# A pre-norm block on one core: first tiles by an uncentred W_in, two idle PSUM banks, three more tiles' statistics on ScalarE

## The chip, the core and the metric

The kernel runs on one core of one Trainium2 chip. A core has TensorE (PE, matrix products), VectorE (DVE), ScalarE (ACT), GpSimd (POOL) and SyncE (SP, which here only issues transfers). The metric is the device time of one execution in microseconds, lower is better.

## The reference

x is 4096 rows of 512, a context is 3202 rows of 1024, a mask has 3202 counts. Two blocks follow each other; everything is float32.

```
h      = rmsnorm(layernorm(x), g_res) @ W_in.T + b_in        # 512 x 512
c      = rmsnorm(context, g_init)[:, :512]
s      = a decaying scan of c along its rows                 # s[i] = a s[i-1] + b c[i]
x      = x + h + s[plug]        # plug: row of s for each row, from the mask's cumulative sums
x      = x + gelu(layernorm(x) @ w1 + b1) @ w2 + b2          # 512 -> 2048 -> 512
```

The layernorm and the rmsnorm in front of W_in are joined: a row's mean is taken out by centring W_in once (the mean over its input rows, weighted with g_res, is subtracted), so the product can be made from raw x, and the scale `ra` of each row is applied afterwards. Each float32 product is made of three float32r products: high x high, high x low, low x high, where a high part is a rounded copy and a low part is the rest.

## The kernel before

The order of work on each engine is written out by hand; engines meet only at semaphores.

The first half runs over 32 tiles of 128 rows (index t, `project(t)`, twelve products each). For a tile: TensorE transposes it in four 128x128 pieces into a bank (`transpose_first`, L847; three banks in turn), ScalarE copies the bank as its high part `h_hi` (`tile_high`, L687), VectorE makes the low part `h_lo` (`tile_low`, L1040), TensorE does the products into one of three banks `p_bank` (L859 to L861), and VectorE adds the scaled result to x (`tile_add`, L1048). Each tile's variance comes from `tile_stats`, on VectorE (L1035, L1036) or, for the tiles in `ON_ACT`, on ScalarE (three ACTIVATEs, L695 to L699); GpSimd makes the scales `ra` for two or four tiles at a time (L519, L520). `project(t)` of TensorE is one step; in ScalarE's and VectorE's loops step t holds the high and low parts of tile t+2, `tile_add(t-1)`, and statistics of a tile further on (t+6 on ScalarE, t+4 on VectorE).

In front of the loop stand 14 warm-up transposes (L887), the column sums of W_in as four fp32 products with a matrix of g_res (`g_wide`, `sum_w_in`, L854), the scaled copies `win_g` (L725), the centring on VectorE (L1140), and W_in's high (L729) and low parts (two on VectorE, L1145, two on GpSimd, L570). All products of the first three tiles wait for these.

Between the tiles lies other work, tied to steps: the mask's cumulative sums and "one-hot" matrices on VectorE (`mask_parts` to `one_hots_p`), which TensorE turns into counts (`mask_totals`, L896; `count_positions`, L902, 26 small products at step 16; `count_before`, L908), the squares and scales of the context on ScalarE (L703 to L712), its multiplication by g_init on GpSimd (L544) after the small loads (`small_loaded`: g_init, b_in, b2, b1), and the scan on VectorE with its carry from TensorE (`carry`, L891, `add_carry`, L1072). PSUM has eight banks: `t_bank` 0 and 1, `h_bank` 0 and 1, `acc` 0 to 3.

The second half does eight groups of 512 rows, 16 pieces of the hidden layer each, TensorE being full; the first group also splits w1 and w2 into parts.

SyncE's queue loads W_in first, then the mask, tiles 2 to 7, context rows and further tiles; ScalarE's queue loads g_res and tiles 0 and 1.

## Time and profile before

| | |
|---|---|
| median of 3 runs | 837.85 us (837.53 to 838.92) |
| profiled execution | 837.43 us, of which the span of the trace is 835.7 us |
| instructions | 10792 |
| TensorE products | 826.4 us busy, 99% of the span |
| VectorE, ScalarE, GpSimd | 315.2, 294.5, 256.3 us busy |

Busy times of TensorE overlap, since each product is recorded from entry to end, so its products are read by the distance between their starts. For the other engines too the distance from one start to the next is what an instruction costs in a full queue; the recorded duration is some 0.1 us longer. "idle before" is the time in which the engine had nothing to do, with what ended it.

### The profile page before, as it was taken

Reading aid. Unit: us, or ns where it says so; the run is one execution under the profiler, and the core shown is the slowest. Engines: PE = TensorE matmul, PEld = TensorE weight load, DVE = VectorE, ACT = ScalarE, POOL = GpSimd, SP = SyncE. Lnnn points to the kernel's source line nnn. Section 1 sums busy time; section 2 is a strip of 40 time slices with the busy share of each in tenths; the row PEclk is TensorE's granted clock in tenths of the full one; section 3 lists DMA queues with packets and bytes.
Section 4 is the critical chain, followed back from the end, with each engine's and each line's share of the span. In section 5 each row is a group of like instructions: output and inputs, shape, how many; then the busy total and the mean of one; then the engine's idle time right before and its main releaser. Section 6 shows DMA issues by size and latency. Waiting matters only on the chain.

```text
span 835.7 us, 10792 instructions
## 1 busy us (share of the span) xinstructions
PE 826.4 (99%) x3770; PEld 680.8 (81%) x3770; DVE 315.2 (38%) x513; ACT 294.5 (35%) x542; POOL 256.3 (31%) x236
## 2 busy tenths in 40 slices
PE   8999999999999999999999999999999999999998
PEld 5887888788888888888888888888888888888886
DVE  6899661664241333233332423143113311242112
ACT  5667446432622253224422262222222322222221
POOL 2273538950533026301631062305300250001000
PEclk9999999999999999999999999999999999999999
DMA  9858984251226022601233113302300230010001
GB/s 239 256 169 276 259 264 179 88 148 27 76 88 174 0 75 77 169 15 66 72 110 89 50 48 113 50 0 102 51 0 1 89 62 0 0 51 0 1 1 50
DMA packets 37327, 74.95 MB, mean 90 GB/s; under 512 B 6176, under 2 KB 6176, under 8 KB 35536
## 3 DMA queue, kind: packets, MB, share of 16 engines
q1 hardware_dynamic: 28324, 62.81, 23.3%
q0 software_dynamic: 4608, 8.39, 6.3%
q10 hardware_dynamic: 4368, 3.42, 1.4%
q8 instruction: 14, 0.23, 0.1%
q14 instruction: 13, 0.11, 0.0%
HBM read 47.87 MB, written 22.84 MB: 85 GB/s over the span
## 4 chain that ended last, share of the span: by engine, by line
PE 85%; POOL 4%; DVE 4%; DMA 2%; issue 2%; SPq 1%; ACT 1%; ACTq 0%; DVEq 0%; POOLq 0%
PE acc L859 14%; PE acc L861 14%; PE acc L860 14%; PE h_bank L859 14%; PE h_bank L861 13%; PE h_bank L860 13%; DMA xa_odd<-in_x_dram 2%; PE t_bank L918 2%; POOL w_lo L525 1%; POOL x_cur L624 1%; POOL cl L544 1%; DVE h_lo L1040 1%; POOL w_lo L531 1%; DVE st_a L1035 1%; SPq L348 0%
## 5 line engine op out<-in xcount | busy, mean ns | idle before, releaser
L1265 DVE TENSOR_TENSOR h_lo<-g_f,h_hi 128x512 fp32r<-128x512 f32 x128 | 99.9, 781 | 430.3 <-ACT g_f L796 420.9
L794 ACT ACTIVATE h_hi<-h_bank,b_c 128x512 fp32r<-128x512 f32 x128 | 88.2, 689 | 430.6 <-PE h_bank L861 425.7
L859 PE MATMUL h_bank<-xt_hi,w_hi 128*128 128x512 f32 x512 | 199.9, 390 | 0.6 <-POOL w_lo L525 0.6
L859 PE MATMUL acc<-w_hi,h_hi 128*128 128x512 f32 x512 | 199.8, 390 | 0.0
L861 PE MATMUL h_bank<-xt_hi,w_lo 128*128 128x512 f32 x512 | 199.3, 389 | 0.0
L860 PE MATMUL h_bank<-xt_lo,w_hi 128*128 128x512 f32 x512 | 199.2, 389 | 0.0
L861 PE MATMUL acc<-w_hi,h_lo 128*128 128x512 f32 x512 | 199.2, 389 | 0.0
L860 PE MATMUL acc<-w_lo,h_hi 128*128 128x512 f32 x512 | 199.2, 389 | 0.0
L859 PEld LDWEIGHTS h_bank<-xt_hi,w_hi 128*128 128x128 f32 x512 | 96.1, 188 | 20.7 <-issue 1.0
L861 PEld LDWEIGHTS h_bank<-xt_hi,w_lo 128*128 128x128 f32 x512 | 96.1, 188 | 20.0
L861 PEld LDWEIGHTS acc<-w_hi,h_lo 128*128 128x128 f32 x512 | 96.1, 188 | 20.0
L860 PEld LDWEIGHTS acc<-w_lo,h_hi 128*128 128x128 f32 x512 | 96.1, 188 | 19.7
L860 PEld LDWEIGHTS h_bank<-xt_lo,w_hi 128*128 128x128 f32 x512 | 96.1, 188 | 19.7
L859 PEld LDWEIGHTS acc<-w_hi,h_hi 128*128 128x128 f32 x512 | 96.1, 188 | 19.7
L796 ACT ACTIVATE g_f<-h_bank,b_c 128x512 f32<-128x512 f32 x128 | 87.4, 683 | 0.4 <-DVE h_lo L1265 0.4
L557 POOL DMA_INDIRECT x_next<-scan_table,idx x32 | 51.4, 1607 | 71.2 <-DMA scan_table<-cl 58.5
L544 POOL TENSOR_TENSOR cl<-cl,g_init_b 128x512 f32<-128x512 f32 x24 | 31.9, 1336 | 98.1 <-ACT ch L705 92.2
L624 POOL TENSOR_TENSOR x_cur<-x_next,b_b 128x512 f32<-128x512 f32 x32 | 44.1, 1408 | 58.4 <-DMA out_dram<-x_cur 58.0
L562 POOL TENSOR_SCALAR va_b<-mv_b 128x4 f32<-128x4 f32 x8 | 1.6, 197 | 176.9 <-DVE mv_b L1171 176.9
L552 POOL TENSOR_TENSOR x_next<-x_next,b_in_b 128x512 f32<-128x512 f32 x32 | 45.7, 1428 | 32.9 <-DMA x_next<-x_part 29.3
L859 PE MATMUL acc<-win_hi,h_hi 128*128 128x512 f32 x88 | 36.8, 418 | 1.8 <-DVE win_lo L1145 1.6
L861 PE MATMUL acc<-win_hi,h_lo 128*128 128x512 f32 x88 | 34.6, 393 | 0.0
(164 smaller groups left out, 695.8 us busy)
## 6 DMA issues: line engine op xcount, KB each, us to landing
out_dram<-x_cur SPq DMA_DIRECT2D x32, 256.0 KB, 2.1
x_next<-x_part SPq DMA_DIRECT2D x7, 1024.0 KB, 5.1
w_raw<-in_L_ffn_w_dram SPq DMA_DIRECT2D x6, 1024.0 KB, 9.1
scan_table<-cl SPq DMA_DIRECT2D x6, 896.0 KB
ch<-in_ctx_dram SPq DMA_DIRECT2D x20, 256.0 KB
cl<-in_ctx_dram SPq DMA_DIRECT2D x5, 1024.0 KB
xa_odd<-in_x_dram SPq DMA_DIRECT2D x16, 256.0 KB, 6.5
x_part<-xa_odd SPq DMA_DIRECT2D x16, 256.0 KB, 4.7
```

The source lines that it names most:

```text
L525: pool.tensor_tensor(w_lo[:, k, r], w_raw[:, k, r], w_hi[:, k, r].bitcast(F32), ALU.subtract).then_inc(w1_ready, 1)
L544: pool.tensor_tensor(rows[:, j, :], rows[:, j, :], g_init_b[:], ALU.mult).then_inc(g_scaled, 1)
L552: step(pool.tensor_tensor(x_next[:, i, :], x_next[:, i, :], b_in_b[:], ALU.add))
L557: pool.indirect_dma_start(x_next[:, i, :], None, rows, bass.IndirectOffsetOnAxis(ap=idx[:, i:i + 1].bitcast(U32), axis=0), compute_op=ALU. ...
L624: ins = pool.tensor_tensor(x_cur[:, i, :], x_next[:, i, :], b2_b[:], ALU.add)
L794: act.activation(h_hi[:, m % HB, :], h_bank[m % 2][:], ACT.Gelu, bias=b1_c[:, m:m + 1])
L796: act.activation(g_f32[:], h_bank[m % 2][:], ACT.Gelu, bias=b1_c[:, m:m + 1]).then_inc(gelu_done, 1)
L859: nc.tensor.matmul(dst, a_hi, b_hi, start=first, stop=False)
L860: nc.tensor.matmul(dst, a_hi, b_lo, start=False, stop=False)
L861: return nc.tensor.matmul(dst, a_lo, b_hi, start=False, stop=final)
L918: ins = nc.tensor.transpose(t_bank[i % 2][:, k * P:(k + 1) * P], n_rows[:, i, k * P:(k + 1) * P], ident[:])
L1265: dve.tensor_tensor(h_lo[:, m % HB, :], g_f32[:], h_hi[:, m % HB, :].bitcast(F32), ALU.subtract).then_inc(h_split, 1)
```

## The change

Tiles 0 to 2 (`RAW = 3`) are projected with a W_in that is scaled by g_res but not centred; it has its own high and low parts, `first_hi` (ScalarE, straight from the loaded block) and `first_lo` (VectorE). What the missing centring leaves is put right by a row operation on VectorE, `fix_tile`: x plus the negated column sums times mean times scale. GpSimd makes the products of mean and scale (`mean_scales`), and now adds up the four scaled blocks (`add_w_in`), so TensorE has one product with a matrix of ones instead of four (`sum_w_in`). ScalarE copies the negated sums to SBUF (`neg_sums`), from where W_in is centred for the tiles from 3 on. All four low parts of W_in are VectorE's. The loads of x tiles 0 to 2 and of W_in are interleaved over both queues. Tiles 3 and 4 are accumulated in `acc[3]` and `h_bank[0]`; `mask_totals`, which uses `h_bank[0]`, moves from step 4 to step 6 and waits for tile 4's add. Tiles 7, 9 and 11 get their statistics on ScalarE. The mask's steps on VectorE move by one (the first by two), the carry of the first context block moves from step 15 to 16 with its adds, warm-ups go from 14 to 10.

```diff
-WARM = 14
+WARM = 10
+RAW = 3
-ON_ACT = (6, 8, 10, 18, 20, 21, 22, 23, 24, 25, 26, 27)
+ON_ACT = (6, 7, 8, 9, 10, 11, 18, 20, 21, 22, 23, 24, 25, 26, 27)
+        def sums_bank(t):
+            return {3: acc[3], 4: h_bank[0]}[t] if t in (3, 4) else p_bank[(t + 2 * (t < 3)) % 3]
...
# SyncE
-            for k in range(K):
+            for t, k in ((0, 0), (1, 3)):
+                sp.dma_start(xa(t), x_v[0, :, t, :]).then_inc(xa_loaded[t], 16)
                 sp.dma_start(win_raw[:, k, :], win_v[:, k, :]).then_inc(win_loaded[k], 16)
+            sp.dma_start(xa(2), x_v[0, :, 2, :]).then_inc(xa_loaded[2], 16)
...
# GpSimd, before scales(0, 2)
-            for k in (2, 3):
-                pool.wait_ge(win_hi_done, k + 1)
-                pool.tensor_tensor(win_lo[:, k, :], win_raw[:, k, :], win_hi[:, k, :].bitcast(F32),
-                                   ALU.subtract).then_inc(win_lo_late, 1)
+            add_w_in(1)
+            add_w_in(2)
+            add_w_in(3)
             scales(0, 2)
+            mean_scales(0, 2)
             scales(2, 2)
+            mean_scales(2, 1)
...
# ScalarE
+            high_first(0)
             tile_high(0)
+            high_first(1)
+            scale_w_in(0)
+            scale_w_in(1)
+            tile_high(1)
+            high_first(2)
+            scale_w_in(2)
+            high_first(3)
+            scale_w_in(3)
+            tile_high(2)
+            act.wait_ge(win_summed, 1)
+            act.activation(neg_sums[:], acc[3][:], ACT.Copy, scale=-1.0).then_inc(neg_sums_made, 1)
             high_w_in(0)
-            tile_high(1)
-            high_w_in(1)
-            tile_high(2)
-            high_w_in(2)
-            high_w_in(3)
             tile_high(3)
+            for k in range(1, K):
+                high_w_in(k)
+            tile_high(4)
+            tile_high(5)
...
-                if 2 <= t < NT - 2:
+                if 4 <= t < NT - 2:
                     tile_high(t + 2)
...
# TensorE
             warm_up()
-            sum_w_in(0)
-            sum_w_in(1)
             transpose_first(0)
-            sum_w_in(2)
-            sum_w_in(3)
+            project_raw(0, 0)
             transpose_first(1)
+            project_raw(0, 1)
+            project_raw(1, 0)
+            project_raw(1, 1)
+            project_raw(0, 2)
+            project_raw(1, 2)
             transpose_first(2)
+            project_raw(0, 3)
+            project_raw(1, 3)
+            sum_w_in()
             transpose_first(3)
+            for k in range(K):
+                project_raw(2, k)
             transpose_first(4)
             for t in range(3, NT):
                 if t + 2 < NT:
                     transpose_first(t + 2)
-                if t == 4:
+                if t == 6:
+                    pe.wait_ge(acc_read, 5)
                     mask_totals()
-                if t == 15:
+                if t == 16:
                     pe.wait_ge(consts_made, 5)
                     carry(0, cl, acc[3][:])
...
# VectorE
+            def fix_tile(t):
+                dve.wait_ge(mean_ra_ready, t + 1)
+                ins = dve.scalar_tensor_tensor(x1(t), neg_sums[:], mean_ra[:, t:t + 1], xa(t), ALU.mult, ALU.add)
+                fixed.append(own.inc(ins))
...
-                for v in (t + LEAD,) if t < 22 else (2 * t - 18, 2 * t - 17) if t < 25 else ():
+                for v in {0: (), 1: (), 2: (4,), 3: (5,)}[t] if t < LEAD else (t + LEAD,) if t < 22 else (2 * t - 18, 2 * t - 17) if t < 25 else ():
```

VectorE before, from tile 2's low part (`h_lo<-acc`) to the statistics of tile 3 (BN_STATS, BN_AGGR); the centring and two low parts of W_in are done by then, and the first add follows soon after:

```order
L1040 TENSOR_TENSOR h_lo<-acc,h_hi 128x512 [waits x_hi]
L1035 BN_STATS st_a<-xa_even 128x6 [waits xa_loaded0]
L1036 BN_AGGR mv_a<-st_a 128x2 [waits dve_self]
L1035 BN_STATS st_a<-xa_even 128x6 [waits xa_loaded1]
L1036 BN_AGGR mv_a<-st_a 128x2 [waits dve_self]
L1040 TENSOR_TENSOR h_lo<-t_bank,h_hi 128x512 [waits x_hi]
L1035 BN_STATS st_a<-xa_even 128x6 [waits xa_loaded2]
L1036 BN_AGGR mv_a<-st_a 128x2 [waits dve_self]
L1035 BN_STATS st_a<-xa_even 128x6 [waits xa_loaded3]
L1036 BN_AGGR mv_a<-st_a 128x2 [waits dve_self]
```

VectorE in the changed kernel, behind the statistics of tile 3: centring (`win_raw<-neg_sums`), low parts of W_in and of tiles 3 to 5, fix rows, first add:

```order
L1194 SCALAR_TENSOR_TENSOR win_raw<-neg_sums,win_g 128x512 [waits win_scaled,neg_sums_made]
L1194 SCALAR_TENSOR_TENSOR win_raw<-neg_sums,win_g 128x512 [waits win_scaled]
L1204 TENSOR_TENSOR win_lo<-win_raw,win_hi 128x512 [waits win_hi_done]
L1194 SCALAR_TENSOR_TENSOR win_raw<-neg_sums,win_g 128x512 [waits win_scaled]
L1204 TENSOR_TENSOR win_lo<-win_raw,win_hi 128x512 [waits win_hi_done]
L1083 TENSOR_TENSOR h_lo<-t_bank,h_hi 128x512 [waits x_hi]
L1194 SCALAR_TENSOR_TENSOR win_raw<-neg_sums,win_g 128x512 [waits win_scaled]
L1204 TENSOR_TENSOR win_lo<-win_raw,win_hi 128x512 [waits win_hi_done] x2
L1083 TENSOR_TENSOR h_lo<-t_bank,h_hi 128x512 [waits x_hi]
L1083 TENSOR_TENSOR h_lo<-acc,h_hi 128x512 [waits x_hi]
L1091 SCALAR_TENSOR_TENSOR x_next<-neg_sums,mean_ra,xa_even 128x512 [waits mean_ra_ready] x3
L1102 SCALAR_TENSOR_TENSOR x_next<-h_bank,ra,x_next 128x512 [waits dve_self,ra_ready,h_used]
```

The centring, which stood in front of the statistics of tiles 0 to 3, now stands behind them, together with all four low parts, the low parts of tiles 3 to 5 and the three fix rows; the first add follows only then.

ScalarE before, from tile 3's high part to tile 7's:

```order
L687 ACTIVATE h_hi<-t_bank 128x512
L740 DMA g_init_b<-in_L_xattn_g_init_dram 128x512
L740 DMA b_in_b<-in_L_xattn_b_in_dram 128x512
L740 DMA b_b<-in_L_ffn_b_dram 128x512
L741 DMA b_c<-in_L_ffn_b_dram 128x16x1
L695 ACTIVATE g_f_59,sum_x<-xa_even 128x512
L697 ACTIVATE sum_x<-sum_x 128x1
L699 ACTIVATE g_f_59,mv_a<-xa_even,sum_x 128x512
L687 ACTIVATE h_hi<-t_bank 128x512
L695 ACTIVATE g_f_59,sum_x<-xa_odd 128x512
```

ScalarE in the changed kernel, from tile 5's high part on (statistics of tile 9 and tile 6's high part at the end):

```order
L719 ACTIVATE h_hi<-acc 128x512
L785 DMA g_init_b<-in_L_xattn_g_init_dram 128x512
L785 DMA b_in_b<-in_L_xattn_b_in_dram 128x512
L785 DMA b_b<-in_L_ffn_b_dram 128x512
L786 DMA b_c<-in_L_ffn_b_dram 128x16x1
...
L727 ACTIVATE g_f_59,sum_x<-xa_odd 128x512
L729 ACTIVATE sum_x<-sum_x 128x1
L731 ACTIVATE g_f_59,mv_a<-xa_odd,sum_x 128x512
L719 ACTIVATE h_hi<-t_bank 128x512
```

The high parts of tiles 4 and 5 moved ahead of the small loads, and the statistics of tiles 6 to 9 stand in one piece behind them, ahead of tile 6's high part; before, a tile's high part stood between any two of them.

## Rows read from the trace of the kernel before

**Rows 1.** The page: busy time of each engine.
```profile
PE 826.4 (99%) x3770; PEld 680.8 (81%) x3770; DVE 315.2 (38%) x513; ACT 294.5 (35%) x542; POOL 256.3 (31%) x236
```

**Rows 2.** Waits of TensorE, 0 to 205 us: total us, times, longest.
```profile
PE h_bank L859 <- POOL w_lo L525: 0.6, 1, 0.6
PE h_bank L908 <- DVE row_tot L1154: 0.2, 1, 0.2
```

**Rows 3.** Timeline of TensorE, 0 to 13 us: start, us, what.
```profile
2.53 3.25 PE L887 MATMUL acc<-ident 128*128 128x128 f32 x14 [2.53 <-POOL iota_p L504]
5.57 2.83 PE L854 MATMUL acc<-win_raw,g_wide 128*128 128x512 f32 x4
8.24 0.60 PE L847 MATMUL t_bank<-ident,xa_even 128*128 128x128 f32 x4
8.68 1.88 PE L854 MATMUL acc<-win_raw,g_wide 128*128 128x512 f32 x4
10.40 0.60 PE L847 MATMUL t_bank<-ident,xa_even 128*128 128x128 f32 x4
...
12.82 0.47 PE L859 MATMUL acc<-win_hi,h_hi 128*128 128x512 f32 x1 [1.39 <-DVE win_lo L1145]
```

**Rows 4.** Timeline of TensorE: transposes of two tiles that follow each other.
```profile
35.90 0.60 PE L847 MATMUL t_bank<-ident,xa_odd 128*128 128x128 f32 x4
...
39.11 0.60 PE L847 MATMUL t_bank<-ident,xa_odd 128*128 128x128 f32 x4
```

**Rows 5.** Timeline of SyncE's queue: issue of W_in's four blocks.
```profile
0.82 1.83 SPq L340 DMA_DIRECT2D win_raw<-in_L_xattn_W_in_dram  x4
```

**Rows 6.** W_in's tile: landings of its four blocks.
```profile
DMA to landing us min/median/max: 3.4/4.7/6.3
```

**Rows 7.** Timeline of VectorE, 15 to 38 us.
```profile
15.59 0.69 DVE L1035 BATCH_NORM_STATS2 st_a<-xa_even 128x6 f32<-128x512 f32 x1
...
16.48 0.67 DVE L1035 BATCH_NORM_STATS2 st_a<-xa_even 128x6 f32<-128x512 f32 x1
...
22.64 0.17 DVE L1078 TENSOR_SCALAR part_i<-mask_i 128x26 int32<-128x26 int32 x1
...
24.33 0.69 DVE L1035 BATCH_NORM_STATS2 st_a<-xa_even 128x6 f32<-128x512 f32 x1
...
34.22 0.75 DVE L1048 SCALAR_TENSOR_TENSOR xa_even<-h_bank,ra,xa_even 128x512 f32<-128x512 f32 x1
34.89 0.68 DVE L1040 TENSOR_TENSOR h_lo<-acc,h_hi 128x512 fp32r<-128x512 f32 x1
...
35.69 1.15 DVE L1101 TENSOR_TENSOR ib<-cum_f,ia 128x26 int32<-128x26 f32 x1
```

**Rows 8.** Timeline of ScalarE, 18 to 34 us.
```profile
18.10 0.60 ACT L687 ACTIVATE h_hi<-t_bank 128x512 fp32r<-128x512 f32 x1 [2.36 <-PE t_bank L847]
...
19.95 0.63 ACT L695 ACTIVATE g_f<-xa_even 128x512 f32<-128x512 f32 x1 [1.25 <-issue]
...
23.15 0.62 ACT L695 ACTIVATE g_f<-xa_odd 128x512 f32<-128x512 f32 x1
...
24.86 0.58 ACT L687 ACTIVATE h_hi<-acc 128x512 fp32r<-128x512 f32 x1
...
32.08 0.62 ACT L703 ACTIVATE ch_all<-ch_all 128x512 f32<-128x512 f32 x1
...
33.45 0.58 ACT L687 ACTIVATE h_hi<-acc 128x512 fp32r<-128x512 f32 x1
```

**Rows 9.** Timeline of GpSimd: two products with g_init.
```profile
33.91 1.30 POOL L544 TENSOR_TENSOR cl<-cl,g_init_b 128x512 f32<-128x512 f32 x1 [3.62 <-DMA b_c<-in_L_ffn_b_dram]
35.48 1.32 POOL L544 TENSOR_TENSOR cl<-cl,g_init_b 128x512 f32<-128x512 f32 x1 [0.27 <-ACT ch_all L705]
```

**Rows 10.** Timeline of VectorE: the second half of the one-hots.
```profile
63.95 1.88 DVE L1128 TENSOR_TENSOR oh_p<-pos_p,iota_p 128x1664 bf16<-128x1664 f32 x1
```

**Rows 11.** Timeline of TensorE: the position counts.
```profile
66.00 0.81 PE L902 MATMUL h_bank<-oh_q,oh_p 128*128 128x32 bf16 x26
```

More of the change, by code:

```diff
@@ L407, in _ @@
             sp.sem_inc(table_stored, STORED)
-            for t in range(2, 8):
+            for t in range(3, 8):
                 load_tile(t)
@@ L567, in _, with add_w_in, mean_scales @@
             pool.sem_inc(consts_made, 1)
-            for k in (2, 3):
-                pool.wait_ge(win_hi_done, k + 1)
-                pool.tensor_tensor(win_lo[:, k, :], win_raw[:, k, :], win_hi[:, k, :].bitcast(F32),
-                                   ALU.subtract).then_inc(win_lo_late, 1)
+            def add_w_in(k):
+                pool.wait_ge(win_scaled, k + 1)
+                src = win_g[:, 0, :] if k == 1 else win_sum
+                ins = pool.tensor_tensor(win_sum, src, win_g[:, k, :], ALU.add)
+                if k < K - 1:
+                    step(ins)
+                else:
+                    ins.then_inc(win_added, 1)
+            def mean_scales(t0, n):
+                pool.wait_ge(ra_ready, t0 + n)
+                u = slice(t0, t0 + n)
+                pool.tensor_tensor(mean_ra[:, u], mv_a[:, u, 0], ra[:, u], ALU.mult).then_inc(mean_ra_ready, n)
+            add_w_in(1)
+            add_w_in(2)
+            add_w_in(3)
             scales(0, 2)
+            mean_scales(0, 2)
             scales(2, 2)
+            mean_scales(2, 1)
             for t in range(NT):
@@ L657, in _ @@
                           allow_slow_non_contiguous=True).then_inc(g_res_loaded, 16)
-            for t in range(2):
-                act.dma_start(xa(t), x_v[0, :, t, :]).then_inc(xa_loaded[t], 16)
+            for k in (1, 2):
+                act.dma_start(win_raw[:, k, :], win_v[:, k, :]).then_inc(win_loaded[k], 16)
             act.sem_inc(gelu_done, CREDIT)
@@ L720, in _, with high_first, scale_w_in @@
             act.wait_ge(g_res_loaded, 16)
-            for k in range(K):
-                act.activation(g_wide[:, k, :], ones[:], ACT.Copy, scale=g_res_c[:, k:k + 1]).then_inc(g_made, 1)
-            for k in range(K):
+            def high_first(k):
                 act.wait_ge(win_loaded[k], 16)
+                act.activation(first_hi[:, k, :], win_raw[:, k, :], ACT.Copy, scale=g_res_c[:, k:k + 1]).then_inc(first_hi_done, 1)
+            def scale_w_in(k):
                 act.activation(win_g[:, k, :], win_raw[:, k, :], ACT.Copy, scale=g_res_c[:, k:k + 1]).then_inc(win_scaled, 1)
@@ L1047, in tile_add @@
                 u = t % XR
-                dve.scalar_tensor_tensor(x1(t), p_bank[t % 3][:], ra[:, u:u + 1], xa(t), ALU.mult, ALU.add).then_inc(acc_read, 1)
+                if t < RAW:
+                    dve.wait_ge(dve_self, fixed[t])
+                rows = x1(t) if t < RAW else xa(t)
+                dve.scalar_tensor_tensor(x1(t), sums_bank(t)[:], ra[:, u:u + 1], rows, ALU.mult, ALU.add).then_inc(acc_read, 1)
             def scan_row(b, rows, j):
@@ L1184, in transposed_low @@
                                   xt_hi[:, :, i * P:(i + 1) * P].bitcast(F32), ALU.subtract).then_inc(t_lo, 1)
+            low_first(0)
             tile_low(0)
+            low_first(1)
+            tile_low(1)
+            low_first(2)
+            tile_stats(0)
+            low_first(3)
+            tile_stats(1)
+            tile_low(2)
+            tile_stats(2)
+            tile_stats(3)
             centre_w_in(0)
@@ L1189, in _ @@
             low_w_in(0)
-            tile_low(1)
             centre_w_in(2)
             low_w_in(1)
+            tile_low(3)
             centre_w_in(3)
-            tile_low(2)
-            tile_stats(0)
-            tile_stats(1)
-            tile_low(3)
-            tile_stats(2)
-            tile_stats(3)
+            low_w_in(2)
+            low_w_in(3)
+            tile_low(4)
+            tile_low(5)
+            for t in range(RAW):
+                fix_tile(t)
             for t in range(NT):
```

85 lines of the change are left out of this document (44 added, 41 removed).

## The prediction

> **What bounds the kernel now.** I read the busy line first: TensorE is busy 99% of the span [rows 1], so a change can only move the time by moving TensorE's gaps or its work. Its waits are few: the first product waits for the low part of W_in, and one wait for VectorE's row counts stands much later; the feed-forward half has a single wait of 0.6 us [rows 2]. TensorE's timeline of the start shows where there is something to win: 14 warm-up transposes, four fp32 products that sum W_in's columns, transposes, and the first real product only at 12.82 us [rows 3]. After some 30 us a tile costs 3.21 us from transposes to transposes (35.90 to 39.11), four transposes taking 0.44 (8.24 to 8.68) and twelve products (3.21 - 0.44) / 12 = 0.23 each [rows 3, 4]; nothing stalls there.
>
> But "TensorE is full" hides that VectorE is nearly full beside it from 10 to 70 us. The view that shows it is VectorE's timeline: between tile 8's low part (34.89) and the second half of the one-hots (63.95, 1.88 long) it hardly rests, and TensorE's position counts, which need that one-hot, start at 66.00, 0.17 after it ends at 65.83 [rows 7, 10, 11]. So at that place there is no slack: if VectorE gets there later, TensorE waits. That is the point from which I work back.
>
> **The change, part by part.** *TensorE's start.* Four warm-ups go (4 x 0.22, from 3.04 us of issue for 14), the fp32 column sums go (8.68 to 10.40 is two, 0.86 each) and one comes back. The first product now needs x tile 0, its two halves, and the uncentred W_in's two halves. W_in's four blocks were issued from 0.82 to 2.65 us, and took 3.4 us (the shortest, which I take as the first) to 6.3 (the last) to land [rows 5, 6]: 4.2 and 8.5. With the requests interleaved, x tile 0 takes the first place (4.2) and W_in block 0 the second of six equal transfers (about 5.4, interpolated). Then high part 0.7 (a copy of this size is 0.60 long, 18.10 [rows 8]; 0.1 for the scale), low part 0.7 and tile 0's low part 0.7 (0.68 each, 34.89 [rows 7]): first product at about 7.6 instead of 12.8. Tile 1's transposes now stand behind that product, so its low part comes at 9.5 and the next products at 10.3. Tile 2's transposes follow at 13.1, the single column sum at 14.9. TensorE would start tile 6's transposes at 23.4 and tile 8's at 29.8, against 35.90 - 3.21 = 32.7 before [rows 4]: 2.9 us ahead. This is the gain that the edit offers.
>
> *VectorE's new work.* Added before the second one-hots: four low parts of the uncentred W_in (4 x 0.60), three fix rows (3 x 0.67, priced like the adds, 34.22 to 34.89; low parts and centrings by 0.60, their distance in a full queue, 34.89 to 35.69 less an instruction of 0.2), two low parts of W_in that were GpSimd's (2 x 0.60): 5.6 us. Removed: three tiles' statistics, 3 x 0.89 (15.59 to 16.48) = 2.7 [rows 7]. Some of the 5.6 falls at the very start, where VectorE had to wait; the rest does not. From tile 2's low part (14.3 by my count) it is dense: that low part 0.6, statistics of tiles 2 and 3 1.8, four centrings 2.4, four low parts of W_in 2.7 with waits, low parts of tiles 3 to 5 1.8, fixes 2.0, adds 0 and 1 1.3, statistics 4 0.9, add 2 0.7, mask parts 1.7 (22.64 to 24.33), statistics 5 0.9, add 3 0.7. That is 17.5 us, and only then, at 31.8, tile 6's low part. TensorE has by then finished tile 5 (29.8) and stands.
>
> *ScalarE's new order is worse.* It can make the last centred high part at 21.2 (VectorE centres block 3 behind tile 3's low part). Then: high part 0.5, tiles 4 and 5 1.0, the issue of four loads 1.3 (18.10 to 19.95 less one copy), and four tiles' statistics in a row, 6 to 9, at 1.71 each (23.15 to 24.86) = 6.8, because steps 0 to 3 have no tile copy any more: tile 6's high part at 30.8. Behind it 0.5, statistics 10 1.7, tile 7 0.5, squares 1.4 (32.08 to 33.45), statistics 11 1.7: tile 8's high part at 36.6, against 33.45 before [rows 8]. So VectorE's low part of tile 8 starts at 37.2 against 34.89: **2.3 us late**.
>
> *The mask sum at step 6.* It is written to a bank that tile 4 now uses and waits for add 4. GpSimd's scale for tiles 4 to 7 waits for statistics 5 (31.1), 1.5 later it is ready, add 4 ends at 33.5; TensorE resumes at 33.6. It had come at 30.2, so it stands 3.4 us, and tile 6's products start 0.6 later than before (32.7 and 0.35 for the transposes). The head start is spent here.
>
> *From tile 8 to the one-hots.* The work on VectorE is the same but for the mask's positions, which move behind this point (+0.5), and statistics 11, which leave (-0.9). 2.3 - 0.4 = **1.9 us** late at the second one-hots, hence also at the position counts, 66.0 becoming 67.9. The first carry a step later costs nothing: its four adds only change places before the row counts, and TensorE's wait there [rows 2] stays as it is. Behind it TensorE is full, the second half included [rows 1, 2], so nothing gives the 1.9 back; loads, stores and gathers move with it. Block 0's store leaves some 5 us later on SP's queue, with x stores and a load behind it; tile loads had landed many us ahead of use, so I put it at 0.
>
> *The clock.* The page's clock line shows no low slice, but the issue of transposes does: (5.57 - 2.53) / 14 = 0.22 us apart in the warm-up, (8.68 - 8.24) / 4 = 0.11 later [rows 3], that is 1.2 and 2.4 GHz, and before the rise TensorE worked without a gap. In the changed kernel it stops at about 5.6 and idles for 2 us. If the rise came no later, the cost is 0; if it came only after tile 2's transposes, everything from 7.6 on is at half rate: five groups of 0.7 and the transposes, of which 1.8 us reach the sum of W_in, since waits hide the rest. I take **0.7**, a rise that is one or two product groups late. The Trainium skill (TensorE: Matmul & The Clock Gate, Part 1) says that the low clock is the default and only activity lifts it, which speaks against cutting warm-ups and leaving a gap; by that rule the cost is above 0.
>
> *The port.* A 26-element add took 1.15 us (35.69) beside GpSimd's 128x512 multiply (35.48, 1.32 long), and both ended at the same time [rows 7, 9]. GpSimd's multiplies wait for the small loads (33.91 before), whose issue moves from 18.1 to 22.7, so they come at about 38 in a row and the mask's carries now meet two instead of one: between 0 and 1.3 us more. I take 0 in the sum and keep 1.3 for the range. The Trainium skill (SBUF, Who interferes with whom) calls this an exclusive lock against VectorE's instructions with two SBUF inputs; by that rule the first low parts and GpSimd's new W_in adds block each other too, but VectorE waits for tile 2 after them anyway.
>
> **The sum.** 1.9 + 0.7 = 2.6 us slower. The profiled execution took 837.43 us (span 835.7), so 840.0; the median of the runs is 0.42 above it, hence **840.5**.
>
> **The rivals.** *A, the head start survives (not slower).* TensorE is 2.9 us ahead at tile 8's transposes; if VectorE and ScalarE kept up, and with the three statistics off VectorE (2.7), it would stay ahead at the one-hots: 837.85 - 2.7 = 835.2. It decides at one point: tile 8's low part must start before 34.89. For it: 5.2 us between old and new first product, and what VectorE waited at the start. Against it: the two sums above, which would both have to be 2.5 us too long, though every duration is measured. *B, a draw.* Some of the waits that I counted (centring behind the column sum, the ScalarE queue) run closer together, and 1 to 2 us are won; VectorE then arrives as before: 838.3. *C, both unknowns fall badly:* 1.9 + 1.8 for the clock + 1.3 for the port = 5.0: 842.9. *D, the mask wait is all:* if the backlog behind tile 8 dissolved, only the 0.6 of tile 6 would stay, 838.5, within B's case.
>
> **Chances.** Forecast 0.56, A 0.09, B with D 0.20, C 0.15. A measurement of this kernel tells 0.2% from no change, 1.7 us: slower begins at 839.5. The forecast's own range is 838.8 to 841.8, of which I count 0.03 to "same", so: slower 0.53 + 0.15 = 0.68, same 0.23, faster 0.09. The range reaches into B and C: 837.2 to 842.9.
>
> **What would show it.** Right: first product near 7.6; a TensorE wait of about 3 us before the mask sum, ended by an add; four statistics in a row on ScalarE, tile 6's high part near 31; VectorE's tile 8 low part near 37; the position counts waiting 1 us or more for the one-hots near 68; transposes of tile 1 still 0.22 apart. Wrong: the mask wait under 1 us, or the counts starting before 66.

## The result, and the profile after

The changed kernel takes 842.66 us (median of 5 runs, 841.72 to 843.55) against 837.85 before (837.53 to 838.92). The ratio is 1.0053, with a 95% interval of 1.0040 to 1.0066: slower, inside the range that was given (837.2 to 842.9) and near its upper end, but above the 838.8 to 841.8 that the forecast itself stood for. The profiled execution took 842.73 us with a span of 840.6, so the trace shows the whole loss: 840.6 - 835.7 = 4.9 us.

The page's line of busy times is nearly that of before [rows 1]; TensorE's busy time, slow products included, is 1.0 us longer, and the other 3.9 of the 4.9 us are time in which it stood:

```profile
PE 827.4 (98%) x3760; PEld 681.7 (81%) x3760; DVE 317.4 (38%) x516; ACT 301.0 (36%) x558; POOL 257.1 (31%) x239
```

TensorE's waits (us in total, times, longest) show one new large wait, in front of the mask sum (L939), which before did not wait at all [rows 2]. The wait for the row counts is gone:

```profile
PE h_bank L939 <- DVE xa_even L1102: 3.2, 1, 3.2
...
PE h_bank L901 <- DVE h_lo L1083: 1.9, 1, 1.9
```

The timeline of TensorE in the changed kernel (start us, duration us, what, and in brackets the idle time before it with its releaser) answers to [rows 3, 4, 11]:

```profile
8.01 0.80 PE L901 MATMUL h_bank<-first_hi,h_hi 128*128 128x512 f32 x1 [1.89 <-DVE h_lo L1083]
...
12.52 0.63 PE L902 MATMUL acc<-first_lo,h_hi 128*128 128x512 f32 x1
12.95 0.63 PE L903 MATMUL acc<-first_hi,h_lo 128*128 128x512 f32 x1
...
14.59 0.39 PE L902 MATMUL h_bank<-first_lo,h_hi 128*128 128x512 f32 x1
14.82 0.40 PE L903 MATMUL h_bank<-first_hi,h_lo 128*128 128x512 f32 x1
...
15.76 0.60 PE L892 MATMUL acc<-ident,xa_even 128*128 128x128 f32 x4
...
32.61 0.60 PE L892 MATMUL acc<-ident,xa_odd 128*128 128x128 f32 x4
36.42 0.39 PE L939 MATMUL h_bank<-part_f,tri 128*128 128x3 f32 x2 [3.21 <-DVE xa_even L1102]
...
38.34 0.63 PE L901 MATMUL acc<-win_hi,h_hi 128*128 128x512 f32 x1
38.77 0.63 PE L902 MATMUL acc<-win_lo,h_hi 128*128 128x512 f32 x1
...
40.90 0.80 PE L892 MATMUL t_bank<-ident,xa_odd 128*128 128x128 f32 x4
...
71.23 0.80 PE L945 MATMUL h_bank<-oh_q,oh_p 128*128 128x32 bf16 x26
```

```profile
34.00:38.00 4.00, 1.58 (x8) 0.99 0.19 69
38.00:42.00 4.00, 4.00 (x14) 0.59 0.80 184
```

Before, the same two stretches read 1.00. What ended the stand is on VectorE, ScalarE and GpSimd, whose timelines answer to [rows 7 to 9]. VectorE:

```profile
34.52 0.68 DVE L1083 TENSOR_TENSOR h_lo<-t_bank,h_hi 128x512 fp32r<-128x512 f32 x1
35.62 0.75 DVE L1102 SCALAR_TENSOR_TENSOR xa_even<-h_bank,ra,xa_even 128x512 f32<-128x512 f32 x1 [0.41 <-POOL ra L535]
...
39.66 0.69 DVE L1083 TENSOR_TENSOR h_lo<-acc,h_hi 128x512 fp32r<-128x512 f32 x1 [2.03 <-ACT h_hi L719]
...
43.84 1.26 DVE L1132 TENSOR_SCALAR cum_i<-ic 128x26 int32<-128x26 int32 x1
...
68.88 1.88 DVE L1182 TENSOR_TENSOR oh_p<-pos_p,iota_p 128x1664 bf16<-128x1664 f32 x1
```

ScalarE (the first two of four sets of statistics, then the high parts of tiles 6 and 8):

```profile
25.91 0.63 ACT L727 ACTIVATE g_f<-xa_even 128x512 f32<-128x512 f32 x1 [0.40 <-issue]
...
27.82 0.64 ACT L727 ACTIVATE g_f<-xa_even 128x512 f32<-128x512 f32 x1
...
33.33 0.58 ACT L719 ACTIVATE h_hi<-t_bank 128x512 fp32r<-128x512 f32 x1
...
39.05 0.57 ACT L719 ACTIVATE h_hi<-acc 128x512 fp32r<-128x512 f32 x1
```

GpSimd (the scales of tiles 4 to 7, and a multiply beside the stretched VectorE instruction at 43.84):

```profile
34.16 0.20 POOL L534 TENSOR_SCALAR va_a<-mv_a 128x4 f32<-128x4 f32 x1 [12.63 <-DVE mv_a L1079]
...
43.78 1.29 POOL L559 TENSOR_TENSOR cl<-cl,g_init_b 128x512 f32<-128x512 f32 x1 [1.43 <-ACT ch_all L737]
```

The order is as foreseen: VectorE's statistics of tile 5, GpSimd's scale, VectorE's addition of tile 4, TensorE's mask sum. W_in's blocks took 4.5 to 7.6 us to land, where they took 3.4 to 6.3 [rows 6]:

```profile
DMA to landing us min/median/max: 4.5/7.0/7.6
```

### The profile page after: what moved, and what is told of

Read it like the earlier page. It is cut to its first block, busy times and chain, and to the rows that moved or that the text cites. A ratio compares the mean times of both kernels' runs of the same rounds, so it can differ in the third digit from the quotient of the medians.

```text
span 840.6 us, 10793 instructions
## 1 busy us (share of the span) xinstructions
PE 827.4 (98%) x3760; PEld 681.7 (81%) x3760; DVE 317.4 (38%) x516; ACT 301.0 (36%) x558; POOL 257.1 (31%) x239
## 4 chain that ended last, share of the span: by engine, by line
PE 91%; POOL 4%; DVE 2%; issue 1%; ACT 1%; DMA 1%; SPq 0%; DVEq 0%; POOLq 0%; ACTq 0%
PE acc L901 15%; PE acc L903 15%; PE acc L902 15%; PE h_bank L901 14%; PE h_bank L903 14%; PE h_bank L902 14%; PE t_bank L961 2%; POOL w_lo L540 1%; PE t_bank L892 1%; POOL x_cur L656 1%; POOL cl L559 1%; POOL w_lo L546 1%; DMA win_raw<-in_L_xattn_W_in_dram 1%; DVE h_lo L1083 0%; PE acc L892 0%
## 5 line engine op out<-in xcount | busy, mean ns | idle before, releaser
L749 ACT ACTIVATE xt_hi<-t_bank 128x512 fp32r<-128x512 f32 x32 | 17.4, 596 | 47.1 <-PE h_bank L903 37.4
L901 PE MATMUL acc<-win_hi,h_hi 128*128 128x512 f32 x76 | 31.9, 420 | 0.6 <-DVE h_lo L1083 0.6
```

The costliest lines, as they stand in the source:

```text
L749: act.activation(xt_hi[:, :, i * P:(i + 1) * P], t_bank[i % 2][:].rearrange("p (k r) -> p k r", k=K), ACT.Copy).then_inc(t_hi, 1)
L901: nc.tensor.matmul(dst, a_hi, b_hi, start=first, stop=False)
```

## The experiments

Twelve kernels were run, each with the ratio to the kernel before on its own chip. Their medians lie close together, so the landmarks of the profiled executions do most of the telling. Each kernel has one profiled execution, which need not lie near its median.

**1. The stand of step 6 filled with idle transposes** (changed kernel).

```diff
+            def fill(n):
+                for _ in range(n):
+                    nc.tensor.transpose(acc[0][:, 0:P], ident[:], ident[:])
...
                 if t == 6:
+                    pe.wait_ge(acc_read, 2)
+                    fill(26)
                     pe.wait_ge(acc_read, 5)
                     mask_totals()
```

> The changed kernel with 26 extra 128-column transposes on TensorE at step 6, where it stands 3.2 us for tile 4's add (their results go to a free bank and are not used). Theory: 1.7 of the 4.9 us come from TensorE's clock, which the trace shows at its lower level from 37.9 to 41.3 us, right behind that stand; kept busy, TensorE keeps the upper level, tile 6's twelve products take 2.7 us again, not 4.5, and the run is 1.0 to 1.7 us faster than the changed kernel's 842.7 (1.0 if VectorE's one-hots then become the later of the two). Rival: the lower level is not tied to the stand, the products stay at 0.43 us, and the time stays at 842.7 or rises.

Measured: 841.30 us, ratio 1.0038 (1.0024 to 1.0052), 1.36 less than the changed kernel. The mask sum comes at 35.26 and tile 9's transposes at 38.34, a distance of 3.08 where the changed kernel has 40.90 - 36.42 = 4.48. So 1.40 us of the loss is the clock behind the stand. The mask sum itself came 1.16 earlier (36.42 to 35.26), and that is not the fill's doing but the start's: in this execution the clock had risen before the pause in front of the first products (they are 0.24 apart, at 8.41 and 8.65), fell again at about 9.2, behind that pause of 2.02 us, and rose at 12.6. Its windows:

```profile
6.00:10.00 4.00, 1.98 (x10) 0.90 0.99 348
10.00:14.00 4.00, 3.87 (x13) 0.67 1.08 286
```

The profiled execution (842.08) is the slowest of the five; it lost 1.4 us of its gain to a wait for `n_rows` ahead of the second half, which the changed kernel does not have.

**2. The pause at the start filled** (changed kernel), ten idle transposes between tile 0's transposes and the first products.

```diff
             transpose_first(0)
+            fill(10)
             project_raw(0, 0)
```

> The changed kernel with 10 extra transposes on TensorE between tile 0's transposes and its first product, where it stands about 2 us (results unused). Theory: the clock is then at its upper level before 8 us instead of 14.0, tile 2's transposes start near 13.9 instead of 15.76, everything behind moves with them and the run is 1.9 us faster (840.8). Rival: the late landing of W_in's blocks (9.4 and 9.6 us) sets the pace of the start, not the clock: under 0.7 us of gain.

Measured: 841.89 us, ratio 1.0046 (1.0032 to 1.0060): only 0.8 less where 1.9 was expected. The first half of the expectation held: tile 2's transposes at 13.78 instead of 15.76, tile 8's at 30.66. The stand then is as long as ever (3.22), and the stretch at the lower clock is twice as long, 6.8 us for 3.4; it begins a microsecond before the stand ends:

```profile
34.00:38.00 4.00, 3.52 (x9) 0.50 0.49 173
38.00:42.00 4.00, 4.00 (x16) 0.72 0.42 90
```

Tile 9's transposes come at 40.19, so 1.2 of the 1.95 won at tile 8 were given back at the stand.

**3. The mask sum out of the way** (changed kernel), to step 7 with positions and carries.

```diff
-                if t == 6:
+                if t == 7:
                     pe.wait_ge(acc_read, 5)
                     mask_totals()
...
-                if t == 6:
-                    mask_positions()
                 if t == 7:
+                    mask_positions()
                     mask_carries()
```

> The changed kernel with the mask's sum on TensorE at step 7 instead of 6 and its use on VectorE in the same step, so that step 6 no longer waits for tile 4's add. Theory (VectorE and ScalarE are behind, the mask sum is only the place where it shows): tile 6's products wait for their low part (35.2) in its place, the stand falls from 3.2 to 2.3 us, the lower clock behind it comes or stays away with the luck of that length: 841 to 842. Rival (the wait for the add is the fault of the change): the stand goes as a whole and with it the lower clock, 3.4 + 1.7 us: 838.

Measured: 842.41 us, ratio 1.0044 (1.0030 to 1.0058). TensorE stood only 2.03, for tile 6's low part, and tile 9's transposes came at 38.06; but it then waited 0.45 for a low part at 62.12 and 1.14 for the one-hots at 70.77, so of the 2.8 us won at tile 9 (40.90 to 38.06) the counts kept only 0.46 (71.23 to 70.77). The rival with 838 us fell; the median is 0.4 above the theory's range.

**4. Ten warm-ups in the kernel before** (`WARM = 10`, nothing else).

> The kernel before with 10 warm-up transposes instead of 14, nothing else. Theory: its column sums follow at once and keep TensorE busy, so the clock rises at the same moment and the time is the same (837.6 to 838.1). Rival (warm-ups are worth something by themselves): the rise comes a few us later and the time is 0.7 us or more longer.

Measured: 838.54 us against 837.81, ratio 1.0004 (0.9995 to 1.0013): no change that can be told, though the median is 0.4 above the range expected. The missing warm-ups cost nothing that shows as long as the column sums follow at once.

The profiled execution took 840.11 us, with a mean granted clock of 1.0, and shows something else. In the kernel before ScalarE's statistics of tile 10 wait for that tile's load; here they could start only 1.5 us later. The row in the kernel before, and below it in this run:

```profile
29.89 0.63 ACT L695 ACTIVATE g_f<-xa_odd 128x512 f32<-128x512 f32 x1 [2.95 <-DMA xa_odd<-in_x_dram]
```

```profile
31.43 0.63 ACT L695 ACTIVATE g_f<-xa_odd 128x512 f32<-128x512 f32 x1 [4.38 <-DMA xa_odd<-in_x_dram]
```

VectorE's low part of tile 8 moved with it, from 34.89 to 36.42, TensorE waited 0.68 and 0.70 for later low parts, and the position counts came at 68.52 instead of 66.00. So the landing of a single load moves VectorE in the kernel before, and 2.6 us of span went with it here (838.3 for 835.7), some of them by a small mask operation that met GpSimd's multiply (three of the 26-element ones are stretched where two were).

**5. Both fills together** (changed kernel with the edits of 1 and 2).

> The changed kernel with both sets of idle transposes: ten behind tile 0's transposes at the start, twenty-six in step 6 ahead of the mask sum (they write a bank that nobody reads then). Theory (two separate clock losses, at the start and behind the stand of step 6, each paid in full when alone): tile 9's transposes at about 37.5 us (40.9 without either, 38.3 with the second alone, 40.2 with the first alone), no low stretch of the clock between 30 and 50 us, and the time 840.6 us (840.0 to 841.3). Rival (VectorE's backlog decides once the clock is mended, so the two do not add): the waits of TensorE for tile lows and one-hots after 40 us grow by what was won, and the time stays at 841.3 us, that of the second set alone.

Measured: 840.93 us, ratio 1.0033 (1.0020 to 1.0047), twelve runs in two groups: six at 839.15 to 839.91, five at 841.95 to 842.23, and one at 844.51. The profiled one took 839.5 with a span of 837.3. TensorE's timeline of that execution, and its window from 38 to 42 us:

```profile
8.30 0.40 PE L902 MATMUL h_bank<-first_lo,h_hi 128*128 128x512 f32 x1
8.54 0.39 PE L903 MATMUL h_bank<-first_hi,h_lo 128*128 128x512 f32 x1
...
13.63 0.60 PE L892 MATMUL acc<-ident,xa_even 128*128 128x128 f32 x4
...
34.29 0.39 PE L939 MATMUL h_bank<-part_f,tri 128*128 128x3 f32 x2 [0.35 <-DVE xa_even L1109]
...
37.37 0.60 PE L892 MATMUL t_bank<-ident,xa_odd 128*128 128x128 f32 x4
```

```profile
38.00:42.00 4.00, 4.00 (x21) 1.00 0.72 186
```

This is the change with its clock mended. The products are 0.23 apart from the start; tile 2's transposes come 15.76 - 13.63 = 2.13 earlier and so does the mask sum (36.42 - 34.29 = 2.13), tile 9's transposes 3.53. The span is 3.3 us shorter. So in these profiled executions, of the 4.9 us lost, 3.3 are the clock's, 2.1 at the start and 1.4 behind the stand (3.5 at tile 9, of which 3.3 reach the end), and 837.3 - 835.7 = 1.6 are the stand itself less what is left of the head start. The two losses add, which was the theory, in the lower group of runs (none of the changed kernel's five runs took less than 841.72). The median, 840.93, is inside the theory's range and only 1.7 us below the changed kernel's. The clock does not part the two groups: its mean is 0.999 or 1.0 in all twelve runs, so the upper group loses some 2.5 us by something else, of which there is no profile.

**6. Both fills, and the mask sum in step 7.**

> The changed kernel with both sets of idle transposes and the mask sum, the mask positions and their carries all in step 7, so that tile 6's products wait only for tile 6's low part. Theory (tile 6's low part at 34.5 is next, with VectorE's queue behind it): tile 9's transposes at about 37 us; VectorE's queue is as long as before, so TensorE waits for a low part or the one-hots by some 1 to 2 us between 45 and 70 us, and the time is 840.5 us (839.8 to 841.3). Rival (the mask sum's place holds the rest): no wait over 0.5 us behind it and the time 838.5 us or less.

Measured: 841.76 us, ratio 1.0041 (1.0028 to 1.0054). Tile 9's transposes at 37.11; behind them TensorE waited 0.32 and 0.39 for low parts and 1.14 for the one-hots, 1.85 in all, as expected, but the time missed its expectation by 0.5 above the range. Moving the mask sum brought nothing here; the comparison is not clean, since this execution also had the long issue that experiment 9 shows.

**7. The three sets of statistics back on VectorE** (changed kernel).

```diff
-ON_ACT = (6, 7, 8, 9, 10, 11, 18, 20, 21, 22, 23, 24, 25, 26, 27)
+ON_ACT = (6, 8, 10, 18, 20, 21, 22, 23, 24, 25, 26, 27)
...
-                for v in {0: (), 1: (), 2: (4,), 3: (5,)}[t] if t < LEAD
+                for v in {0: (), 1: (), 2: (4,), 3: (5, 7)}[t] if t < LEAD
```

> The changed kernel with the statistics of tiles 7, 9 and 11 back on VectorE, as the kernel before has them. Theory (VectorE's queue ahead of the mask sum sets the stand in step 6): one more set of statistics, 0.87 us, stands before tile 4's addition, the stand of TensorE grows from 3.2 to about 4.0 us, and the time is 843.4 us (842.8 to 844.2). Rival (the longer queue of ScalarE is what makes the low parts late): tile 8's high part comes 1.9 us earlier, the stand stays, and the time falls to 841.7 us or less.

Measured: 846.51 us, ratio 1.0099 (1.0083 to 1.0114), 3.9 more than the changed kernel. The stand grew to 4.50, and TensorE waited 0.51 for a low part and 1.14 for the one-hots. The sign was the theory's, the size was more than four times the 0.8 expected. Its second one-hot starts at 72.95 instead of 68.88, 4.1 later: three sets of statistics are 2.6 us, where the expectation counted one, and VectorE's small mask operations met three of GpSimd's multiplies instead of two, about 1.0 us more each (1.25, 1.27 and 1.18 long, and 0.18 alone). So moving the statistics was needed to bear VectorE's other new work.

**8. The same line alone in the kernel before** (`ON_ACT` with 7, 9 and 11).

> The kernel before with one line of the change: statistics of tiles 7, 9 and 11 on ScalarE. Theory (ScalarE has little slack in the first 40 us, VectorE hardly waits in it): the high parts of tiles 5 to 8 come up to 1.7 us later, TensorE waits for one of them by 0 to 1 us, and the time is 838.1 us (837.6 to 838.9). Rival (VectorE's relief of 3 x 0.87 us is worth something by itself): 837.3 us or less, with tile 20's transposes earlier than before.

Measured: 839.36 us against 838.04, ratio 1.0015 (1.0006 to 1.0023). That is 0.5 above the range expected. The line costs a little in the kernel before: tile 8's low part comes at 36.13 instead of 34.89, behind ScalarE's high part, and four small mask operations are stretched where two were (1.27, 1.18, 1.18 and 1.25 us), so VectorE's relief of 2.6 us is used up. TensorE waits for two low parts, which it did not before, the first of them here and the second, 0.38, at 57.07:

```profile
50.03 0.50 PE L859 MATMUL h_bank<-win_hi,h_hi 128*128 128x512 f32 x1 [0.98 <-DVE h_lo L1040]
```

**9. Both fills, without the three fix rows** (the rows of tiles 0 to 2 lack the correction for the mean).

```diff
-            for t in range(RAW):
-                fix_tile(t)
...
-                rows = x1(t) if t < RAW else xa(t)
+                rows = xa(t)
```

> The changed kernel with both sets of idle transposes and without VectorE's three operations that correct the rows of tiles 0 to 2 for the mean (2.07 us in all at 26.4 us), so those rows lack the correction. Theory (the amount of VectorE's new work ahead of tile 4's addition sets the stand, us for us): the mask sum comes 2.1 us earlier than with both sets alone (34.3 to about 32.2), tile 9's transposes at 35.3 us, tile 22's at 80.3 against 82.4, and the fastest runs fall from 839.5 to 837.4 us, even with the kernel before. Rival (another engine's wait, ScalarE's statistics and high parts, stands right behind): less than 0.7 us of it arrives and the fastest runs stay above 838.8 us.

Measured: 841.59 us, ratio 1.0037 (1.0023 to 1.0052), no run under 840.97. The theory's time was missed: 2.07 us less on VectorE, and the mask sum stood at 34.40 where it had stood at 34.29. VectorE arrived early and waited for ScalarE instead, first for tile 6's high part:

```profile
32.99 0.69 DVE L1090 TENSOR_TENSOR h_lo<-t_bank,h_hi 128x512 fp32r<-128x512 f32 x1 [2.44 <-ACT h_hi L719]
```

ScalarE was itself 1.17 us later than in experiment 5 (tile 6's high part at 32.38 for 31.21), by one instruction: the issue of b1's load. Its row in this kernel, and below it in experiment 5:

```profile
23.37 1.54 ACTq L786 DMA_DIRECT2D b_c<-in_L_ffn_b_dram  x1
```

```profile
23.29 0.46 ACTq L786 DMA_DIRECT2D b_c<-in_L_ffn_b_dram  x1
```

So the profiled execution differs from experiment 5's in two things, and it does not tell how much of VectorE's 2.07 us would have arrived without the long issue. By these rows about half: with tile 6's high part 1.17 earlier VectorE would have waited 1.3 for it and not 2.44. The rival, ScalarE right behind VectorE, holds for the rest.

The issue was long (1.45 to 1.58 us) in the profiled executions of experiments 2, 6, 9 and 10, which all have the ten transposes at the start, and 0.46 in all others, experiment 5 among them. It is not a matter of the moment alone: it began at 23.33 us in experiment 11 and was short, and at 23.37 here. With it, high parts and squares slide by a microsecond against GpSimd's multiplies, and the number of VectorE's small operations that meet one changes: one in the profiled executions of experiments 1, 5 and 11, two here, three in experiment 10, at about 1.0 us each. This may be what parts the two groups of experiment 5; that was not tested, and a late landing as in experiment 4 is a rival.

**10. The same work in another order** (changed kernel with the ten transposes at the start; the mask's later steps and the counting, not shown, move by one or two steps).

```diff
-                if t + 6 in ON_ACT:
-                    tile_stats(t + 6)
+                for v in {4: (6, 7, 8), 5: (9, 10), 6: (11,)}.get(t, (t + 6,) if t > 6 else ()):
+                    if v in ON_ACT:
+                        tile_stats(v)
...
+                if t == 1:
+                    tile_stats(4)
+                    tile_stats(5)
+                if t == 3:
+                    tile_low(6)
-                if 4 <= t < NT - 2:
+                if 5 <= t < NT - 2:
                     tile_low(t + 2)
-                if t == 3:
+                if t == 4:
                     mask_parts()
```

> The changed kernel with the ten idle transposes at the start, and the same work in another order: ScalarE's high part of tile 6 ahead of its statistics and those of 9 to 11 spread behind it, VectorE's statistics of tiles 4 and 5 behind tile 0's addition, tile 6's low part ahead of the mask parts, the mask sum in step 7, positions, carries and places together in step 8, the counting a step later. Nothing is added or left out. Theory (VectorE's amount of work, not its order, is the limit): no stand over 1 us in step 6 and tile 9's transposes at about 34 to 35 us, but TensorE then waits for low parts of tiles 11 to 14 and for the one-hots, tile 22's transposes come at about 82 us and the time is 840.5 us (839.3 to 841.8). Rival (the order made the stand, VectorE has slack later): waits behind step 7 stay under 1 us in sum, tile 22's transposes at 79 us and the time 836.5 us.

Measured: 843.42 us, ratio 1.0056 (1.0043 to 1.0070), 3 us over the 840.5 expected. The stand is gone, as expected; TensorE then stands later:

```profile
30.66 0.60 PE L893 MATMUL acc<-ident,xa_odd 128*128 128x128 f32 x4
...
33.87 0.60 PE L893 MATMUL t_bank<-ident,xa_odd 128*128 128x128 f32 x4
...
49.99 0.50 PE L902 MATMUL h_bank<-win_hi,h_hi 128*128 128x512 f32 x1 [1.86 <-DVE h_lo L1089]
...
81.80 1.13 PE L935 MATMUL acc<-cl_next,band 128*128 128x512 f32 x2 [1.57 <-DVE cl L1132]
```

and behind the wait of 1.86 us the clock falls once more, which the expectation had not priced:

```profile
50.00:54.00 4.00, 4.00 (x11) 0.62 0.46 135
```

This order is no better, which fits the theory that the amount of work beside TensorE is the limit; one order, in an execution with the long issue and three stretched mask operations, does not prove it.

**11. Fourteen warm-ups in the changed kernel** (`WARM = 14`).

> The changed kernel with fourteen warm-up transposes as before instead of ten. Theory (the late rise of the clock comes from TensorE's pause between tile 0's transposes and the first products, 2.8 us of it): tile 0's transposes at about 5.6 us, the pause stays 2 us or more, the products behind it are still 0.43 us apart up to about 12 us, and the time stays at 842.7 us (842.0 to 843.4). Rival (the four warm-ups that were taken away delayed the rise): the first products 0.23 us apart from the start, tile 2's transposes at 13.8 us instead of 15.8, and the time 841.7 us or less.

Measured: 842.54 us, ratio 1.0050 (1.0036 to 1.0063), so the median is the theory's. But the five runs are not alike: four at 842.13 to 843.32, with a mean granted clock of 0.995 to 0.996, and one, the profiled one, at 839.38 with a clock of 1.0. That one contradicts the theory's reason: the pause is there (1.75), the stand is there (3.18), and neither costs any clock. It shows all three signs of the rival: first products 0.23 apart (8.32 and 8.55), tile 2's transposes at 13.66, and a time under 841.7. Its clock had risen before the pause (tile 0's four transposes took 0.67 us, and 1.12 in the changed kernel). So the four warm-ups may decide in some executions; in four of five they were not enough.

```profile
7.98 0.50 PE L901 MATMUL h_bank<-first_hi,h_hi 128*128 128x512 f32 x1 [1.75 <-DVE h_lo L1083]
8.32 0.40 PE L902 MATMUL h_bank<-first_lo,h_hi 128*128 128x512 f32 x1
...
34.34 0.38 PE L939 MATMUL h_bank<-part_f,tri 128*128 128x3 f32 x2 [3.18 <-DVE xa_even L1102]
...
37.42 0.60 PE L892 MATMUL t_bank<-ident,xa_odd 128*128 128x128 f32 x4
```

The windows of the same execution in which the clock of the changed kernel and of experiment 2 is low:

```profile
34.00:38.00 4.00, 3.66 (x19) 1.00 0.56 178
38.00:42.00 4.00, 4.00 (x22) 1.00 0.69 186
```

A mean clock of 0.996 over 840 us is 0.004 x 840 = 3.4 us of full clock lost, and 839.4 + 3.4 = 842.8, where the other four are. The same kernel pays the clock or not from one execution to the next. In this kernel most executions paid. The mean clock is no exact bill, though: a low clock during a stand costs nothing, one ahead of the first recorded change is not in it, and of the changed kernel's own runs the fastest (841.72) has 0.995 and the slowest (843.55) 0.998.

This execution is also the second measure of what the clock costs: without any fill its landmarks (34.34, 37.42) and its span (837.2) are those of experiment 5 (34.29, 37.37 and 837.3).

**12. The first carry a step later, in the kernel before.**

```diff
-                if t == 15:
+                if t == 16:
                     pe.wait_ge(consts_made, 5)
                     carry(0, cl, acc[3][:])
```

(and VectorE's two halves of its addition in steps 16 and 17)

> The kernel before with one part of the change: TensorE's first carry product in step 16 and VectorE's two halves of its addition in steps 16 and 17 instead of 15 and 16. Theory (it lies beside other work on both engines): the same time as before, 837.9 us (837.4 to 838.5), tile 22's transposes at 80.9 us. Rival (the later block delays the second carry product in step 19 or the counting): TensorE waits for the block by 0.5 us or more there and the time is 838.5 us or more.

Measured: 837.84 us, ratio 0.9993 (0.9984 to 1.0002), beside 839.14 for the kernel before, whose fifteen runs there fell in two groups too, at 837.3 to 838.4 and at 839.1 to 839.8: no change, as priced. A wait of 0.17 before the second carry product is all that it left.

No version that was tried beats the kernel before; the best profiles of the changed kernel, those of experiments 11 and 5, are still 1.5 and 1.6 us behind it in span.

## Why the prediction was right, and which term was wrong

*Direction and chain.* Slower was forecast with 0.68, and it is slower through the chain that was named: VectorE's backlog, statistics of tile 5, GpSimd's scale, the addition of tile 4, the mask sum. The stand was put at 3.4 us and is 3.21. VectorE's list from tile 2's low part to tile 6's was put at 17.5 us and takes 34.52 - 17.02 = 17.5; only its start, 14.3 by the prediction, was 2.7 late. Four sets of statistics in a row hold up ScalarE's tile 6; one behind the other they cost 27.82 - 25.91 = 1.91 and not the 1.71 read off [rows 8], 33.33 - 25.91 = 7.4 us in all for 6.8. Rival A (the head start survives) and B with D (a draw, or only 0.6 us at tile 6) fell: tile 8's low part starts at 39.66, and not before 34.89.

*The clock is the term that was mis-sized.* It was taken as 0.7 us with bounds of 0 and 1.8. The profiled executions of experiments 5 and 11 put it at 3.3 us of span (3.5 at tile 9), against 1.7 us between the medians of experiment 5 and the changed kernel, where something else holds up half of experiment 5's runs. There are two reasons. At the start, the prediction held that waits would hide most of a late rise. They hid nothing: with the clock mended tile 2's transposes come 2.13 us earlier, and the same 2.13 reach the mask sum. Second, only a late rise was priced, and not a fall. The forecast had a stand of 3.4 us in its own sum and did not ask what a stand does to the clock behind it; it costs 1.40 there (experiment 1). The Trainium skill (TensorE: Matmul & The Clock Gate, Part 1) has the array fall back to its lower clock after idling, so the prediction's own stand called for a term of this kind. The traces agree in part: the clock fell at waits of 3.21 (the changed kernel), 3.22, 4.50 and 1.86 us (experiments 2, 7 and 10) and behind the pause of 2.02 at the start of experiment 1, while behind 2.03 (experiment 3) and 3.18 (the profiled execution of experiment 11) there was no fall. The length of the wait alone does not decide it.

*What is left when the clock is taken out.* The prediction without its clock term was 1.9 us slower; experiment 5 against before has 1.6 in span. The terms beside the clock were right in sum, which is in part luck, since within them two errors cancelled. The head start at tile 8's transposes is 32.7 - 30.50 = 2.2 us in experiment 5 and not 2.9, and tile 9's transposes came 37.37 - 35.90 = 1.47 late, while 0.6 was expected for tile 6. Tile 8's low part, put at 37.2, starts at 37.54 there. On the other side the backlog did not reach the one-hots as a loss of its own: in the changed kernel the counts (71.23) follow the carry product at 70.37 without a wait, since TensorE, 5 us late already, had given VectorE time to catch up. So in the changed kernel the place at which the loss is fixed is the stand, and not the counts, which were put at 67.9 with a wait of 1 us or more. That wait is real in experiments 3, 6, 7 and 9 (1.11 to 1.14), where TensorE comes earlier or VectorE later.

*The small terms.* The first carry at 0: experiment 12. The warm-ups at nothing by themselves: experiment 4, in the kernel before only. The first product at 7.6: 8.01, since the loads landed later than thought (ScalarE's wait for W_in's first block ended at 5.85, where 5.4 was interpolated). That tile loads had landed many microseconds ahead of use was wrong for the kernel before, whose ScalarE stood 2.95 us for tile 10's (experiment 4); in the changed kernel ScalarE comes later and that wait is gone, so the term stays 0. The port at 0: VectorE's mask work met two multiplies (1.26 at 43.84 and 1.03 at 47.27) where before it met three (1.15, 1.27 and 1.43), so nothing was added in this execution; the other versions met one to three, so the term is not a constant. "Transposes of tile 1 still 0.22 apart" was named as the sign of the late clock; the whole first stretch until 14 us has it.

*Rival C,* both unknowns at their bound, gave 842.9 and is nearest in number, but its mechanism is half wrong: the port gave nothing, and the clock alone gave more than its bound in the profiled executions.

*What stays open.* Why the clock falls behind the same stand in most executions and not in all; what makes the upper group of experiment 5, and whether it is the long issue of b1's load, a late landing, or the number of stretched mask operations.

## What to carry to other kernels

A stand of TensorE can be charged twice, once for itself and once for the lower clock behind it, here 3.2 and 1.4 us; price both. Idle transposes in the stand took the second part away. A head start that is won by giving VectorE and ScalarE more to do is worth only what these two can follow: follow both queues to the first place where TensorE needs them, since shortening one (experiment 9) showed the other behind it. When changes of 0.2% are compared, look at each run's mean granted clock, at the landing of single loads and at single long instructions in the queues before a median is explained.

## What the runs showed of the hardware

- The lower clock behind a stand: TensorE's products 0.43 us apart for 3.4 us behind a wait of 3.21 us, twice as long in experiment 2, and 0.62 of the full clock from 50 to 54 us behind a wait of 1.86 us in experiment 10. It is not certain to come: 3.18 us without it in one execution of experiment 11.
- A load's issue of 0.46 us on ScalarE's queue took 1.45 to 1.58 us in four of the fourteen profiled executions, and ScalarE's next instruction came 1.39 to 1.53 us after the one before it had ended, where that gap is 0.40 with the short issue. Why is open.
- A VectorE instruction of 26 elements took 1.26 us (43.84) beside a GpSimd multiply that began 0.06 earlier (43.78, 1.29 long). It has one input, and its like took 0.18 elsewhere. The Trainium skill (SBUF — State Buffer, Who interferes with whom) lets such a one-input operation, where its operands allow it, enter a mode that takes the ports it shares with GpSimd, and this row agrees with it.
